# Expert choice: results stored by plain indirect DMA in one zero-filled buffer per expert, and added to x in SBUF

## What is computed

```python
x = x + _L1_ffn_ref(_layernorm(x), Wr, W1, b1, W2, b2)

N, E = 8192, 8                             # tokens, experts
k = ceil(N * 2.0 / E)                      # 2048 tokens for each expert
scores = softmax(xt @ Wr, axis=-1)
G, idx = top_k(scores.T, k)                # each expert chooses its tokens
X_in = xt[idx]
h = gelu(einsum('ekd,edh->ekh', X_in, W1) + b1, approximate=False)
X_e = einsum('ekh,ehd->ekd', h, W2) + b2
out = zeros((N, D)).at[idx.reshape(-1)].add((G[..., None] * X_e).reshape(E * k, D))
```

## Time and profile before

| | |
|---|---|
| three runs | 4754.3, 4758.47 (median), 4760.33 us |
| profiled execution, its time | 4758.95 us |
| its span, first to last instruction | 4757.2 us |
| mean granted clock of PE | 0.913 of full speed |
| busy in the span | PE 3840.2 us (81%), DVE 3015.1 (63%), ACT 1850.1 (39%), POOL 1536.8 (32%) |
| second stage (ternary FFN) | about 893 to 1072 us |
| fourth stage: router from 1736, choice from 1801, first gather 1892.3, last scatter's end 2315.7, end 2334 us | |

### The profile page before, as it was taken

The page is one execution under the profiler, slowest core; times in us unless marked ns, Lnnn a source line. Parts: engine busy times, 40 slices in busy tenths (PEclk is TensorE's granted clock), DMA queues, the critical chain, the costliest instruction groups (busy, mean ns, idle before and its releaser), DMA issues. The chain is left out here.

```text
span 4757.2 us, 73605 instructions
## 1 busy us (share of the span) xinstructions
PE 3840.2 (81%) x24747; PEld 2430.0 (51%) x24802; DVE 3015.1 (63%) x6927; ACT 1850.1 (39%) x3217; POOL 1536.8 (32%) x1244
## 2 busy tenths in 40 slices
PE   4999999786999973777477776777759999998579
PEld 2777777565777762444233333333326666664234
DVE  5555555455666646333299999999976666665932
ACT  1555555423555530222254544544533223222222
POOL 2111111252111100688466656666640100100300
PEclk9999999897999975888789998898989999999689
DMA  5233332004334330233312112112110000000000
GB/s 130 68 70 74 74 72 61 6 0 94 89 93 94 91 120 18 39 43 43 83 61 64 61 51 66 56 54 65 55 65 1 1 0 0 0 0 6 0 19 22
DMA packets 196267, 238.72 MB, mean 50 GB/s; under 512 B 35411, under 2 KB 148405, under 8 KB 185702
## 3 DMA queue, kind: packets, MB, share of 16 engines
q1 hardware_dynamic: 170406, 216.50, 17.3%
q0 software_dynamic: 22528, 17.32, 2.7%
q10 hardware_dynamic: 3040, 1.15, 0.1%
HBM read 178.21 MB, written 55.51 MB: 49 GB/s over the span
## 5 line engine op out<-in xcount | busy, mean ns | idle before, releaser
L410 DVE TENSOR_REDUCE a_Mx<-a_Sx 128x2 f32<-128x512 f32 (+1 forms) x1024 | 591.9, 618 | 452.9 <-PE a_Sx L461 259.0
L2011 POOL TENSOR_TENSOR a_inp<-a_dtu,a_Bs 128x512 f32<-128x512 f32 x512 | 662.6, 1325 | 247.9 <-DVE a_h L2154 201.2
L339 ACT ACTIVATE a_Pr<-a_Se 128x512 f32<-128x512 f32 (+1 forms) x1024 | 527.7, 542 | 510.6 <-PE a_Se L484 288.4
L2154 DVE TENSOR_TENSOR_SCAN a_h<-a_dA,a_inp 128x512 f32<-128x512 f32 x512 | 597.6, 1204 | 57.3 <-POOL a_inp L2011 31.8
L2244 PE MATMUL a_Y<-a_hc,g_ident 128*128 128x512 f32 x1024 | 529.8, 643 | 13.7 <-DVE a_hc L2163 13.3
L2077 ACT ACTIVATE a_dA<-a_dtA,a_A 128x512 f32<-128x512 f32 x512 | 342.5, 687 | 424.1 <-DVE a_h L2154 423.6
L284 POOL TENSOR_TENSOR a_rest<-a_qk,a_parts 128x512 f32<-128x512 f32 x64 | 74.2, 1160 | 1118.3 <-ACT a_parts L315 1118.3
L461 PE MATMUL a_Sx<-a_Kp,a_Qp 96*128 96x256 bf16 (+1 forms) x2048 | 377.2, 263 | 14.2 <-DMA a_Kp<-a_packing 11.6
L1819 ACT ACTIVATE f_sg<-f_GB 128x512 f32<-128x512 f32 x272 | 162.6, 598 | 511.5 <-PE f_GB L1869 511.3
L1764 DVE TENSOR_TENSOR f_sg<-f_sg,f_UB 128x512 f32<-128x512 f32 x256 | 176.2, 688 | 281.6 <-PE f_CB L1876 271.3
L1902 PEld LDWEIGHTS f_OUT<-f_wd,f_hm 128*128 128x128 f32 x2176 | 287.0, 192 | 91.3 <-issue 82.1
(11 more groups left out here) (417 smaller groups left out, 7954.3 us busy)
## 6 DMA issues: line engine op xcount, KB each, us to landing
a_Bs<-a_brows SPq DMA_DIRECT2D x256, 256.0 KB, 3.2
a_Qp<-a_packing SPq DMA_DIRECT2D x192, 192.0 KB
a_Kp<-a_packing SPq DMA_DIRECT2D x192, 192.0 KB
a_packing<-a_parts SPq DMA_DIRECT2D x64, 384.0 KB
a_packing<-a_parts SPq DMA_DIRECT2D x64, 128.0 KB
g_x<-x SPq DMA_DIRECT2D x8, 512.0 KB, 7.4
f_sum<-g_x SPq DMA_DIRECT2D x1, 4096.0 KB, 12.3
f_w<-L_w SPq DMA_DIRECT2D x2, 2048.0 KB
```

The source lines that it names most:

```text
L339: nc.scalar.activation(Pr[h % NP][:, 0:K0Q + K1Q], Se[h % 2][:, 0:K0Q + K1Q], ACT.Exp).then_inc(s["exp_done"], 1)
L410: nc.vector.tensor_reduce(Mx[(k + 2 - (j < LATE)) % 2][:, t, 2 * jj:2 * jj + 2], Sx[t][:, 0:2 * wd].rearrange("p (h q) -> p h q", h=2), AX ...
L2011: nc.gpsimd.tensor_tensor(inp[n % Q][c][:], dtu[k][:, c], Bs[n % Q][:], ALU.mult)\
L2154: nc.vector.tensor_tensor_scan(h[n % 2][c][:], dA[bank[2 * n + c]][:], inp[n % Q][c][:], 0.0, ALU.mult, ALU.add).then_inc(s["scanned"], 1)
```

## The change

The results of expert e go to a DRAM buffer of its own, res["spread"][e], 8192 x 128 float32. Eight such buffers, 32 MB in all, are filled with zeros during the second stage: POOL clears a tile of 128 x 4096, and SP writes it sixteen times. The scatter has no addition and POOL no wait between experts. SP reads each expert's buffer back as two halves of 2 MB once its stores have landed, and DVE adds each half to x in the third and fourth group of the next expert. The last expert's buffer is read in eight parts, as before; DVE adds the even ones, POOL the odd ones, and bn_stats follow. The copy of x to DRAM is gone.

```diff
@@ ternary_ffn
+        blank = sc.sb("blank", [P, TILES * D // 2])
+        @block.sync
+        def _(sp):
+            sp.wait_ge(blank_ready, 1)
+            for spread in res["spread"]:
+                flat = spread.rearrange("(p t) d -> p (t d)", t=TILES)
+                for i in range(2):
+                    sp.dma_start(flat[:, i * TILES * D // 2:(i + 1) * TILES * D // 2], blank[:]).then_inc(blanked, 16)
+            sp.wait_ge(blanked, 16 * 2 * len(res["spread"]))
         @block.gpsimd
         def _(q):
+            nc.gpsimd.memset(blank[:], 0.0).then_inc(blank_ready, 1)
             q.wait_ge(half_ready, 1)
@@ expert_choice
         def loads(sp):
-            sp.dma_start(sum_v, x[:]).then_inc(copied, 16)
@@ sync
-                for i in range(NY):
-                    sp.wait_ge(added[i], 64 * len(range(i, GROUPS_E, NY)))
-                for i in range(8):
-                    sp.dma_start(x[:, 8 * i:8 * i + 8], sum_v[:, 8 * i:8 * i + 8]).then_inc(back[i], 16)
+                for e in range(E):
+                    for i in range(NY):
+                        sp.wait_ge(stored[i], 64 * len(range(i, QUARTERS * (e + 1), NY)))
+                    if e < E - 1:
+                        for h in range(2):
+                            wait(sp, summed, 2 * (e - 1) + h + 1)
+                            sp.dma_start(got[:, HALF * h:HALF * h + HALF], spread_v[e][:, HALF * h:HALF * h + HALF])\
+                                .then_inc(fetched[h], 16)
+                    else:
+                        sp.wait_ge(summed, 2 * (E - 1))
+                        for i in range(8):
+                            sp.dma_start(got[:, 8 * i:8 * i + 8], spread_v[e][:, 8 * i:8 * i + 8]).then_inc(back[i], 16)
@@ gpsimd
-                g.wait_ge(copied, 16)
                 def scatter(n):
-                    e = n // QUARTERS
                     g.wait_ge(scaled, G * (n + 1))
-                    if e and n % QUARTERS == 0:
-                        for i in range(NY):
-                            g.wait_ge(added[i], 64 * len(range(i, n, NY)))
                     for t in range(G):
                         nc.gpsimd.indirect_dma_start(
-                            sum_d, bass.IndirectOffsetOnAxis(ap=idx[:, n, t:t + 1], axis=0), Y[n % NY][:, t], None,
-                            compute_op=ALU.add).then_inc(added[n % NY], 16)
+                            res["spread"][n // QUARTERS], bass.IndirectOffsetOnAxis(ap=idx[:, n, t:t + 1], axis=0),
+                            Y[n % NY][:, t], None).then_inc(stored[n % NY], 16)
+                g.wait_ge(summed, 2 * (E - 1))
+                for i in range(1, 8, 2):
+                    g.wait_ge(back[i], 16)
+                    xs = x[:, 8 * i:8 * i + 8]
+                    nc.gpsimd.tensor_tensor(xs, xs, got[:, 8 * i:8 * i + 8], ALU.add).then_inc(eased, 1)
@@ vector, behind the scaling of group n
+                        if n >= QUARTERS and n % QUARTERS >= 2:
+                            h = n % QUARTERS - 2
+                            v.wait_ge(fetched[h], 16 * e)
+                            xs = x[:, HALF * h:HALF * h + HALF]
+                            wait(v, summed, 2 * (e - 2) + h + 1)
+                            nc.vector.tensor_tensor(xs, xs, got[:, HALF * h:HALF * h + HALF], ALU.add)\
+                                .then_inc(summed, 1)
                 for i in range(8):
                     v.wait_ge(back[i], 16)
+                    xs = x[:, 8 * i:8 * i + 8]
+                    if i % 2:
+                        v.wait_ge(eased, i // 2 + 1)
+                    else:
+                        v.wait_ge(summed, 2 * (E - 1) + i // 2)
+                        nc.vector.tensor_tensor(xs, xs, got[:, 8 * i:8 * i + 8], ALU.add).then_inc(summed, 1)
+                        v.wait_ge(summed, 2 * (E - 1) + i // 2 + 1)
                     for t in range(8 * i, 8 * i + 8):
                         nc.vector.bn_stats(res["stats"][:, t, :], x[:, t, :])
```

More of the change, by code:

```diff
@@ L715, in ternary_ffn @@
         half = sc.sb("half", [P, G])
+        blank = sc.sb("blank", [P, TILES * D // 2])
+        blank_ready, blanked = sc.sem("blank_ready"), sc.sem("blanked")
         xn = [sc.sb(f"xn{i}", [P, G, D]) for i in range(2)]
@@ L1163, in expert_choice @@
     rows_d = nc.dram_tensor(name + "_rows", [N, ROW], F32, kind="Internal").ap()
-    sum_d = nc.dram_tensor(name + "_sum", [N, D], F32, kind="Internal").ap()
     rows_v = rows_d.rearrange("(p t) c -> p t c", t=TILES)
-    sum_v = sum_d.rearrange("(p t) c -> p t c", t=TILES)
+    spread_v = [d.rearrange("(p t) c -> p t c", t=TILES) for d in res["spread"]]
     with ExitStack() as outer:
@@ L1173, in expert_choice @@
         crow, span = so.sb("crow", [TILES, E, P + 3], BF16), so.sb("span", [TILES, E, 2])
-        big, copied = so.sem("big"), so.sem("copied")
+        big = so.sem("big")
         def loads(sp):
-            sp.dma_start(sum_v, x[:]).then_inc(copied, 16)
             for dst, src in ((w1, "w1"), (w2, "w2"), (b1, "b1"), (b2, "b2"), (iota, "iota"), (slot, "slot")):
@@ L1193, in expert_choice @@
             junk = sc.sb("junk", [P, G, P])
+            HALF = TILES // 2
+            got = sc.sb("got", [P, TILES, D])
             idx = sc.sb("idx", [P, GROUPS_E, G], mybir.dt.uint32)
@@ L1206, in expert_choice @@
             gathered = [sc.sem(f"gathered{i}") for i in range(NX)]
-            added = [sc.sem(f"added{i}") for i in range(NY)]
+            stored = [sc.sem(f"stored{i}") for i in range(NY)]
+            fetched = [sc.sem(f"fetched{i}") for i in range(2)]
+            summed, eased = sc.sem("summed"), sc.sem("eased")
             back = [sc.sem(f"back{i}") for i in range(8)]
@@ L1311, in _ @@
                         if n >= NY:
-                            v.wait_ge(added[n % NY], 64 * (n // NY))
+                            v.wait_ge(stored[n % NY], 64 * (n // NY))
                         for t in range(G):
@@ L2295, in program @@
                "ones": sc.sb("ones", [P, P]),
+               "spread": [nc.dram_tensor(f"spread{e}", [TILES * P, D], F32, kind="Internal").ap() for e in range(8)],
                "ident_in": a["c_ident"], "identb_in": a["c_identb"], "out": out}
```

## The result

The changed kernel took 4784.06 us (median of 5, 4780.33 to 4787.15) where the kernel before took 4758.47 (median of 5, 4754.3 to 4762.24): ratio 1.0053, 95% interval 1.004 to 1.0067. It is 26 us slower (0.5%); the forecast was 4681 us, with a range up to 4712. Its profiled execution took 4786.74 us for a span of 4785.0.

What follows compares the result with a forecast made beforehand. The prediction took POOL's issue time as the path from 1934 to 2315.7 us. It summed 4758.5 - 12.3 - 65.2 - 9.1 + 3 + 6 = 4680.9, predicted 4681 us, range 4665 to 4712.

Steps and rivals of the forecast that it cites:

- Scatter without addition: Expert stage, POOL: a plain scatter takes 0.979 us instead of 1.583, saving 65.2 us over 27 groups.
- the tail: End of the expert stage: from gather 31 to the last scatter's end 30.2 us instead of 39.3, saving 9.1.
- PE, where nothing holds it, does a group in 8.54 us: Expert stage: PE's pace read from 1932.60 to 1941.14, leaving 1.7 us spare in POOL's new period of 10.2.
- if PE follows: Expert stage: condition on the 65.2 us saving, that PE keeps up with POOL's shorter period.
- 8 us of cover against a single late group: Expert stage: a group is scaled 32.5 us behind its gather, POOL comes to its scatter after 41 us.
- Rival 1: Expert stage: PE becomes the pace; 4697 us at 10.8 us a group, 4713 at 11.4; chance 16%.
- Contention: Expert stage: DVE's adds slow POOL's issue by +3 us, between 0 and 6.7 at the share 0.08 / 0.74.
- The rival that I gave 6%: Expert stage: the adds stop POOL for their whole length, 14 x 4.44 = 62 us; 4740 us; chance 6%.
- Zero fill: Second stage: POOL's memset (at most 3.6 us) and SP's 33.5 MB of writes (104 us) are hidden, cost 0.
- Router: Router stage: without the copy of x, DVE's stall falls from 18.7 to about 6.4 us, saving 12.3.
- Read-back: Last read-back: DVE's adds and waits before four blocks cost +6 us, bounds 4.9 and 9.

Runs made afterwards that it cites:

- run d: The kernel before with only its scatter made plain, without addition: 4669.24 us, 0.9838 of the kernel before.
- standard run: The changed kernel with its 14 adds cut to one element and its fetches to 512 bytes, in the fourth group of runs: 4756.4 us (0.999).
- j: As the standard run, but xg filled by plain DMAs that SP issues, rows in order, POOL issuing scatters alone: 4636.5 us (0.9735).
- second group: Runs including the changed kernel and the kernel before again, both unaltered: 4725.57 us (0.9956) and 4750.12 us (1.0001).
- sixth group: Its run: the changed kernel with adds and fetches cut away as in the standard run, and POOL's scatter one group later: 4752.59 us (0.9986).

## Why the prediction was wrong

**Scatter without addition, -65.2, and the tail, -9.1.** The price was right: 983 ns measured, and 78.2 us less between first and last scatter in run d, against 74.3. In the first measurement the same step gave about 381.5 - 376.1 = 5 us (376.1 is the standard run of the fourth group, the nearest run with late signals and without adds; it has no fetches either). The step that failed is that PE follows: "PE, where nothing holds it, does a group in 8.54 us", and from it "if PE follows" and "8 us of cover against a single late group". The pace itself is right, j shows 8.54 us in 26 rounds. But in the first measurement something holds PE, and the cover is none: in 19 of the 32 groups POOL waits for Y and starts its scatter 1.4 us behind the start of the scaling. PE was held in the very trace that I read: the earlier trace rows shows its first two free turns at 1932.60 and 1941.14, 40 us behind the first gather for the earlier, where the kernel before needs 26.6 in the second group. I read the pace of the turns and not their place. The scalings there were up to 2.8 us late, too; with a period of 12.65 us most scatters stood 10 to 15 us behind the start of their scaling and hid it. That is why the slow scatter lost only 12 us by the late signals (4760 against 4748) and the changed kernel 60 (4785 against 4726). What the kernel before loses lies ahead of its first scatter (41.9 us from the first gather for 28.2). A change that makes the bound resource faster spends the slack of all the others. Rival 1 (PE becomes the pace) names the place but not the size: it stopped at 11.4 us a group, for the clock's sake.

**Contention, +3.** Measured 52 us without late signals, and 408.0 - 376.1 = 32 with them, adds and fetches together, where POOL has idle time to lose. The failed step is the scaling by a share, 0.08 / 0.74 us from the earlier trace rows. A wait of all or nothing doesn't scale so: that gather was already underway when the 0.74 us instruction began, and a row in which POOL came second was not looked for. There was one, the scatter at 2216.97 shown above: of the 0.40 us that were left of the DVE instruction it lost 0.27. The rival that I gave 6% is the one that happened. Its 62 us are 52 because the held DMA comes 0.1 to 1.3 us behind the add's start and ends 0.82 to 0.87 us behind its end, a little less than its own length: 3.7 us an add and not 4.4. The Trainium skill (SBUF — State Buffer, "Who interferes with whom") says this of a DVE instruction with two SBUF inputs and a GpSimd one that reads SBUF, that whoever comes first shuts the other out. The trace agrees for a DVE that comes first (4.92 us for 0.98), with an indirect DMA as the GpSimd instruction. It doesn't for a DMA that comes first: the add behind it kept its 4.41 us. Whether POOL waits to read the index tile or to make the descriptors no run separates.

**Zero fill, 0.** The transfer was hidden as forecast, and quicker: 425 GB/s on average from 905 to 975 us, in place of 323, and done before 980 (second group). The memset was not: I named POOL as the one that might be late and gave 3.6 us, while the one that is held is DVE, and the 3 us stand on the path.

**Router, -12.3.** Measured -10.4 (145.2 for 155.6 us), so 2 us were taken too many. DVE's stall went to 9.06 us and not to 6.4.

**Read-back, +6.** Measured +7.3 (25.2 for 17.9 us); DVE's adds took up to 2.44 us beside POOL's, inside the bound of 9.

**The sum.** Without late signals (second group, d for the scatter): -10.4 - 78.2 + 54.4 (359.6 - 305.2) + 4.9 (second stage, 183.7 - 178.8) + 7.3 = -22.0, measured -22.3. In the first measurement: -10.3 - 5.4 + 31.9 + 2.2 + 7.5 = +25.9, measured +25.6. That both close to 0.3 us is luck: the terms are from profiled executions, whose spans differ by -25.8 and +27.8, and the kernel before varies by 2.6 us in the second stage alone. Of the 103 us between forecast and result, about 69 are the scatter's gain that PE didn't let through, 29 the adds with their fetches, 5 the rest; the split between the first two leans on the standard run of another group. Without late signals the sign would have been right and the size 55 us off, nearly all of it the adds.

## What to carry to other kernels

An elementwise DVE instruction on SBUF beside a POOL that issues indirect DMAs should be short: cut into eight adds of 128x512, the fourteen adds cost 12.6 us (320.1 for 307.5) and not 52, at 0.5 us more of DVE time each. With the adds and the memset cut in this way (g) the kernel is faster than both, the one before and the changed one: 0.9865 of the kernel before without late signals, 0.9981 with them. A pace that was never seen in the trace has to be asked of every engine, by the place of its first turns as well as by their distance, and a contention is priced by a row in which the second comer waits, not by a share.

## What the runs showed of the hardware

- The plain indirect scatter of 128 rows of 512 bytes is issued in 0.97 us, nearly as a gather (0.95); the accumulating one in 1.57 (medians). Put back into the changed kernel the addition costs 69.8 us (429.4 for 359.6) in 128 scatters.
- An indirect DMA that comes to its start while DVE does an add of 128x4096 waits until its end (56 of 56), one already underway doesn't.
- Late signals: with indirect gathers of POOL in flight, PE's semaphore updates reach DVE and ACT late in some groups of runs and in others never, on the same chip: up to 5 us in the rounds of the standard run, 7 in the sixth group, 9 beside the first twenty gathers, and 11 to 13 with fetches. Outside this stage the same groups show nothing of it: behind it the changed kernel takes 2427 us in its first profile and 2429 in the second group's.
- In the groups with late signals the trace itself has holes here. The DMA view from 1892 to 1930 us, first of the kernel before as first profiled, then of the same kernel in the second group:

```profile
f3e_xg<-f_rows,f3e_idx POOLq DMA_INDIRECT x20
```

```profile
f3e_xg<-f_rows,f3e_idx POOLq DMA_INDIRECT x22, 2.5
f_sum<-f3e_Y,f3e_idx POOLq DMA_INDIRECT x4, 3.3
```

  The first has no time to landing, because landings are missing: between 1885 and 2200 us there are 1553 landing records in the one and 3151 in the other. The first stands in the earlier trace rows, and could have been a warning. Lost records and late signals go together in all profiles of this case: 978 to 1588 landing records in this stretch of the profiles with late signals, 3005 to 4033 in those without. The Trainium skill (NOTIFIC — the notification-queue block, "Overflow: three behaviours, one of which stalls the engine") says that the queues which take such records can drop them or stall the engine that makes them. That the recording is what holds PE would fit; no run here separates it, since each was recorded, and what the kernels take unrecorded is open.
